# A batch's norm scalars computed on the scalar engine instead of the vector engine

## The reference

```python
def _gn(v, G=32, eps=1e-5):
    g = v.reshape(B_, G, C_ // G, H_, W_)
    m = jnp.mean(g, axis=(2, 3, 4), keepdims=True)
    s = jnp.var(g, axis=(2, 3, 4), keepdims=True)
    return ((g - m) / jnp.sqrt(s + eps)).reshape(v.shape)

def _L0_conv_ref(x, W, b):
    u = jnp.mean(x, axis=1, keepdims=True)
    s = jnp.sqrt(jnp.var(x, axis=1, keepdims=True, ddof=1))
    n_x = (x - u) / (s + EPS)
    n_x = jnp.einsum('bchw,oc->bohw', n_x, W) + b[None, :, None, None]
    return x * n_x

x = x + _L0_conv_ref(_gn(x), L0_conv_W, L0_conv_b)
```

## Time and profile before

| | us |
|---|---|
| median of 3 runs | 1923.73 (1922.91 to 1929.28) |
| the profiled execution | 1922.92 |
| its span, first to last instruction | 1921.1 |

### The profile page before, as it was taken

How to read it: one execution, slowest core, us unless ns; L and a number is a source line. 1 busy time by engine, 2 the same in 40 slices (tenths; PEclk the granted TensorE clock), 3 DMA queues, 4 the chain that set the end, 5 groups by cost and what they waited for, 6 DMA issues and landing times.

```text
span 1921.1 us, 67613 instructions
## 1 busy us (share of the span) xinstructions
PE 1709.8 (89%) x28706; PEld 924.4 (48%) x28706; DVE 1727.3 (90%) x2120; ACT 1434.4 (75%) x2498; POOL 1458.6 (76%) x1684
## 2 busy tenths in 40 slices
PE   0079998999889998999989999899999999899998
PEld 0045554555445554555545555455545555455553
DVE  5669998999899998999989998999989999888887
ACT  5588885888768986888859888588877888544442
POOL 0067877888778887888878887788878888688885
PEclk9989999999999999999999999999999999999999
DMA  9979998999989998999989999899999999845675
GB/s 378 404 292 347 381 387 304 393 391 394 330 322 416 381 399 332 343 400 379 394 312 383 387 392 376 286 408 388 388 348 330 411 376 388 309 188 198 252 276 221
DMA packets 184188, 671.63 MB, mean 350 GB/s; under 512 B 20688, under 2 KB 21072, under 8 KB 183888
## 3 DMA queue, kind: packets, MB, share of 16 engines
q1 hardware_dynamic: 110160, 398.85, 56.1%
q10 hardware_dynamic: 73728, 268.47, 35.0%
HBM read 398.80 MB, written 268.44 MB: 347 GB/s over the span
## 4 chain that ended last, share of the span: by engine, by line
PE 60%; DVE 18%; DMA 10%; issue 6%; POOL 3%; SPq 2%; ACT 2%; POOLq 0%; ACTq 0%; DVEq 0%
PE proj_ps L732 35%; PE sums_ps L720 13%; PE factor_ps L706 11%; DMA tiles<-x 6%; DVE scaled L630 5%; DVE bn L674 4%; DVE bn L675 4%; DMA out<-tiles 4%; SPq L412 2%; DVE tiles L643 2%; POOL tiles L445 1%; POOL tiles L456 1%; DVE gn L584 1%; ACT squares L528 1%; ACT unused L513 0%
## 5 line engine op out<-in xcount | busy, mean ns | idle before, releaser
L732 PE MATMUL proj_ps<-scaled,w_t 128*32 128x512 f32 x8192 | 993.6, 603 | 0.1
L456 POOL TENSOR_SCALAR tiles<-tiles,out_shift 128x1024 f32<-128x1024 f32 x512 | 577.5, 1128 | 241.7 <-DVE tiles L643 239.0
L643 DVE SCALAR_TENSOR_TENSOR tiles<-proj_ps,gate_shift,tiles 128x1024 f32<-128x1024 f32 x512 | 643.8, 1257 | 72.1 <-PE proj_ps L732 70.6
L445 POOL TENSOR_SCALAR tiles<-tiles,norm_scalars 128x1024 f32<-128x1024 f32 x512 | 618.9, 1209 | 58.7 <-DMA tiles<-x 57.7
L513 ACT ACTIVATE unused<-tiles,bn 128x1024 uint8<-128x1024 f32 x560 | 635.0, 1134 | 0.9 <-DMA tiles<-x 0.9
L630 DVE TENSOR_TENSOR scaled<-tiles,factor_ps 128x1024 f32<-128x1024 f32 x512 | 619.3, 1210 | 8.7 <-PE factor_ps L706 3.9
L528 ACT ACTIVATE squares<-tiles 128x1024 f32<-128x1024 f32 x512 | 538.1, 1051 | 112.0 <-POOL tiles L445 66.3
L706 PE MATMUL factor_ps<-pieces,pick_sb 128*128 128x128 bf16 x4096 | 318.1, 221 | 100.8 <-DVE scaled L630 84.6
L720 PEld LDWEIGHTS sums_ps<-tiles,const_sb 128*32 128x32 f32 x8192 | 247.7, 111 | 318.5 <-issue 277.4
L732 PEld LDWEIGHTS proj_ps<-scaled,w_t 128*32 128x32 f32 x8192 | 214.6, 109 | 363.3 <-issue 309.3
L706 PEld LDWEIGHTS factor_ps<-pieces,pick_sb 128*128 128x128 bf16 x4096 | 231.9, 98 | 210.8 <-DVE scaled L630 103.4
(11 more groups left out here) (56 smaller groups left out, 727.4 us busy)
## 6 DMA issues: line engine op xcount, KB each, us to landing
tiles<-x SPq DMA_DIRECT2D x760, 512.0 KB, 10.0
out<-tiles ACTq DMA_DIRECT2D x512, 512.0 KB, 7.0
const_sb<-const SPq DMA_DIRECT2D x1, 193.5 KB, 2.4
scaled<-w SPq DMA_DIRECT2D x1, 64.0 KB, 2.1
scaled<-ident SPq DMA_DIRECT2D x1, 64.0 KB, 2.2
pick_sb<-pick SPq DMA_DIRECT2D x1, 8.0 KB, 2.2
bias_sb<-bias SPq DMA_DIRECT2D x1, 0.5 KB, 2.2
```

What stands on the lines that cost most here:

```text
L445: nc.gpsimd.tensor_scalar(place(s), place(s), norm_scalars[:, 0:1], norm_scalars[:, 1:2], ALU.add, ALU.mult).then_inc(normed, 1)
L456: nc.gpsimd.tensor_scalar(place(s), place(s), 1.0, out_shift[:, 0:1], ALU.mult, ALU.add).then_inc(finished, 1)
L643: nc.vector.scalar_tensor_tensor(out=place(s), in0=proj_ps[:, s % 2, :], scalar=gate_shift[:, 0:1], in1=place(s), op0=ALU.add, op1=ALU.mul ...
L732: mm = nc.tensor.matmul(proj_ps[q:q + 32, s % 2, h:h + BANK], w_t[:, q:q + 32], scaled[:, s % 2, h:h + BANK], start=True, stop=True)
```

## The change

The one-column chain moves to ScalarE, except its first two operations and two reciprocals. VectorE's `gather` (`bn_aggr` and `reduce_sum`) runs at the end of step 58, since `GN_STEP` becomes 58. ScalarE's `moments` (eight operations) runs in step 59 behind the squares and ahead of the store; `deviation` (two) in step 61 behind the root, ahead of the store; `spread_of_group` (eight) in step 62 behind the squares and ahead of the `piece` operations. VectorE's `invert_root` runs in step 62 where part 2 was, and `invert_std` where part 3 was. The two matmuls stay at steps 61 and 62 and read other columns. The epsilon is a column of its own in the constants.

```diff
-        GN_STEPS = 19
-        GN_STEP = slots - 5
+        GN_STEPS = 18
+        GN_STEP = slots - 6
@@ GpSimd, norm, slot 0
                     pool.wait_ge(gn_step, (batch + 1) * GN_STEPS)
+                    pool.wait_ge(inv_std_done, batch + 1)
@@ ScalarE
+            def gn_then(instruction, n, done):
+
+                instruction.then_inc(gn_step, 1)
+                act.wait_ge(gn_step, n * GN_STEPS + done)
+
+            def moments(n, of):
+
+                total = slots * SLOT
+                bn_part = of.bn_slots / slots
+                act.wait_ge(gn_gathered, 2 * n + 2)
+                gn_then(nc.scalar.activation(cell(4), cell(0), ACT.Identity, bias=pivot_of(of), scale=-1.0), n, 1)
+                gn_then(nc.scalar.activation(cell(5), cell(4), ACT.Identity, bias=cell(1), scale=cell(4)), n, 2)
+                gn_then(nc.scalar.activation(cell(6, 2), cell(2, 2), ACT.Copy, scale=1.0 / total), n, 3)
+                gn_then(nc.scalar.activation(cell(8), cell(4), ACT.Identity, bias=cell(6), scale=bn_part), n, 4)
+                gn_then(nc.scalar.activation(cell(9), cell(5), ACT.Identity, bias=cell(7), scale=bn_part), n, 5)
+                gn_then(nc.scalar.activation(cell(10), cell(8), ACT.Copy, scale=-1.0), n, 6)
+                gn_then(nc.scalar.activation(cell(11), cell(8), ACT.Identity, bias=pivot_of(of), scale=-1.0), n, 7)
+                gn_then(nc.scalar.activation(cell(4), cell(8), ACT.Identity, bias=cell(9), scale=cell(10)), n, 8)
+
+            def deviation(n):
+
+                act.wait_ge(group_mean_done, n + 1)
+                gn_then(nc.scalar.activation(cell(5), small_ps[:, 0:1], ACT.Identity, bias=cell(11), scale=-1.0), n, 9)
+                gn_then(nc.scalar.activation(cell(12), cell(5), ACT.Identity, bias=cell(4), scale=cell(5)), n, 10)
+
+            def spread_of_group(n):
+
+                act.wait_ge(group_var_done, n + 1)
+                gn_then(nc.scalar.activation(cell(8), small_ps[:, 1:2], ACT.Relu), n, 11)
+                gn_then(nc.scalar.add(cell(9), cell(8), at["gn_eps"]), n, 12)
+                gn_then(nc.scalar.activation(cell(13), cell(9), ACT.Sqrt), n, 13)
+                gn_then(nc.scalar.activation(neg_mean, small_ps[:, 0:1], ACT.Copy, scale=-1.0), n, 14)
+                if n > 0:
+                    act.wait_ge(out_shift_set, n)
+                gn_then(nc.scalar.activation(mean, small_ps[:, 0:1], ACT.Copy), n, 15)
+                act.wait_ge(gn_inverse_done, n + 1)
+                gn_then(nc.scalar.activation(cell(10), cell(14), ACT.Identity, bias=cell(13), scale=cell(9)), n, 16)
+                gn_then(nc.scalar.activation(cell(15), cell(10), ACT.Copy, scale=0.5), n, 17)
+                if n > 0:
+                    act.wait_ge(gate_shift_set, n)
+                gn_then(nc.scalar.activation(gate_new, cell(15), ACT.Identity, bias=bias_sb[:, 0:1]), n, 18)
...
@@ VectorE (gn_scalars goes)
+            def gather(n, of):
+
+                dve.wait_ge(bn_done, bn_before(n) + of.bn_slots)
+                nc.vector.bn_aggr(gn[:, 0:2], bn_of(of)[:, 0:2 * of.bn_slots, :].rearrange("p a b -> p (a b)"))\
+                    .then_inc(gn_gathered, 1)
+                dve.wait_ge(act_done, act_before(n) + 2 * of.act_slots)
+                nc.vector.reduce_sum(gn[:, 2:4], act_sums[:, :, 0:of.act_slots], AXIS_X).then_inc(gn_gathered, 1)
+
+            def invert_root(n):
+
+                dve.wait_ge(gn_step, n * GN_STEPS + 13)
+                nc.vector.reciprocal(gn[:, 14:15], gn[:, 13:14]).then_inc(gn_inverse_done, 1)
+
+            def invert_std(n):
+
+                dve.wait_ge(gn_step, n * GN_STEPS + 17)
+                nc.vector.reciprocal(inv_std, gn[:, 15:16]).then_inc(inv_std_done, 1)
...
@@ VectorE, gate, slot 0
+                            dve.wait_ge(gn_step, (b + 1) * GN_STEPS)
                             nc.vector.tensor_copy(gate_shift[:, :], gate_new).then_inc(gate_shift_set, 1)
@@ TensorE
-                    if nxt and step == GN_STEP + 2:
-                        pe.wait_ge(gn_step, (b + 1) * GN_STEPS + 9)
+                    if nxt and step == GN_STEP + 3:
+                        pe.wait_ge(gn_step, (b + 1) * GN_STEPS + 8)
...
-                    if nxt and step == GN_STEP + 3:
-                        pe.wait_ge(gn_step, (b + 1) * GN_STEPS + 11)
+                    if nxt and step == GN_STEP + 4:
+                        pe.wait_ge(gn_step, (b + 1) * GN_STEPS + 10)
```

73 lines of the change are left out of this document (19 added, 54 removed).

## The result

The changed kernel takes 1909.87 us in the median of six runs (1906.89 to 1913.88), the kernel before 1923.32 in six beside them (1922.17 to 1929.28): ratio 0.9928, with an interval of 0.9913 to 0.9944. It is faster, by 13.5 us. The profiled execution takes 1910.8 us with a span of 1909.0, 12.1 under the span of before; the forecast was 8.8 under.

The account below looks back on a forecast made before the run. The prediction took TensorE's waits at the seven batch boundaries as what an edit could shorten. Its terms, -12.1 + 2.1 - 1.3 + 3.5 - 3.4 + 2.4, gave -8.8 us: a median of 1915 us, forecast 1908 to 1920, full range 1905 to 1930.

Parts of the forecast that it names:

- Step 60, -12.1: TensorE's gap before step 60, waiting for VectorE's scaled slot, goes whole at all seven boundaries: -12.1 us.
- Steps 54 to 59, +2.1: The gather now stands before step 59's scaling; TensorE waits 1.05 us more at the first and third boundary: +2.1 us.
- Steps 62 and 63, -1.3: VectorE's gain before step 63 is nearly all lost to ScalarE's longer queue before `pieces`: -0.2 us a boundary, -1.3.
- ScalarE's prices: One-column operations on ScalarE: 188 ns without a pointer operand, 108 ns more per pointer, 33 ns between dependent ones.
- The store, +3.5: Step 59's store, issued behind `moments`, delays the last streamed slot's normalization: 0.5 us a boundary, +3.5 us.
- the late store decides: Rival, chance 0.12: the late load and normalization of the last streamed slot at step 62 make the kernel slower, 1932 us.
- The clock, -3.4: Clock falls after the gap before step 60, at three boundaries, 1.7 us each, lose their cause; two counted: -3.4 us.
- the rival that had more of it: Rival, chance 0.14: less idle time also ends the clock falls after load waits just before step 59: 1907 us.
- The start, +2.4: Before the first normalized slot nothing hides the longer chain and the square root's table load of 1.28 us: +2.4 us.
- Given back to DMA (0.19): Rival, chance 0.19: time won at boundaries returns as GpSimd's load waits in steps 54 to 58: 1922 to 1926 us.
- the rival of table loads in each batch: Rival, chance 0.04: two table loads of 1.28 us enter each batch's chain at step 62: 1929 us.
- Two signs of being wrong: GpSimd waiting for the load of the batch's last slot; a gap before step 59 at more than two boundaries.

Follow-up runs that it names:

- moments_back: The changed kernel with the eight operations of `moments` back on VectorE at the end of step 59, the gather left in step 58: 1916.64 us, ratio 0.9961.
- after_again: The changed kernel measured once more, unedited: 1910.84 us, ratio 0.9913.
- reorder: The changed kernel with step 62 reordered on GpSimd, ScalarE and VectorE, the fit's pieces first and `invert_std` behind step 63's scaling: 1896.68 us, ratio 0.9844.
- store_late: The changed kernel with the store of step 59 issued two steps later, behind step 61's squares: 1917.94 us, ratio 0.9969.
- store_first: The changed kernel with the stores of steps 59 and 61 ahead of `moments` and `deviation` in ScalarE's queue: 1908.02 us, ratio 0.9901.
- before_filled: The kernel before with six extra projection matmuls on TensorE in front of step 60's spread: 1924.14 us, ratio 1.0.
- table_early: The changed kernel with one extra one-column square root as ScalarE's first instruction, loading its table early: 1903.11 us in one run.

## Why the prediction was right, and where a term was off

**Step 60, -12.1: right.** The gap went whole at every boundary. The column gives -11.0, since at the seventh the clock fell one step earlier, to 0.71 of 2.4 GHz on the mean of the five us shown above, and step 59 took 4.90 us there instead of 3.28 (+1.6). The second execution doesn't have it (23.0, -12.6 against before). `moments_back` ties the gap to the operations. Part of the gap had a cause that the forecast didn't see: at the fourth and the fifth boundary one operation of the seven took 1.10 and 1.11 us instead of 0.17 (last section).

**Steps 54 to 59, +2.1: +1.2 and +1.5 in the two executions**, in a column with more noise than that. At the first boundary TensorE's wait is 1.21 us where it was 0.71, with VectorE's scaled slot as its releaser: the mechanism is as forecast, with 0.5 us for the 1.05. That releaser stands at the first and the fifth boundary, not the third, and at none in `after_again`. So the gather's price is not measured; the gather alone at step 58 was not tried.

**Steps 62 and 63, -1.3: -1.9.** TensorE starts step 63 at z + 4.66 (z + 4.62 by the prediction's z), against z + 4.7 in the forecast, and GpSimd's `pieces` release it. What I missed on the way is VectorE's idle time before `invert_root`: 2.48 us and not 0.8. I counted it from z, but VectorE is through with its scaling 1.7 us earlier, at 312.07. It costs nothing as long as `pieces` are later than the scaled slot, and `reorder`, in which they are earlier, moves that operation too, so no run shows what it would cost there.

**ScalarE's prices: right within 20 ns.** Groups of ScalarE after, one column with two pointers, with one, and two columns without:

```profile
L535 ACT ACTIVATE gn<-gn 128x1 f32<-128x1 f32 x8 | 3.1, 387 | 0.3
...
L553 ACT ACTIVATE gn<-gn,const_sb 128x1 f32<-128x1 f32 x8 | 2.4, 294 | 0.3
...
L536 ACT ACTIVATE gn<-gn 128x2 f32<-128x2 f32 x8 | 1.6, 203 | 0.3
```

Worked out for one column they were 404, 296 and 188 ns. The page of the Trainium skill named in the prediction, "ScalarE: Activation LUTs" (section "What ACT_TABLE_LOAD costs"), has 93 ns for a pointer; the trace has (387 - 203) / 2 = 92 and agrees.

**The store, +3.5: 0 in the two executions. This is the term that was mis-sized.** The first half of the step holds: the store of step 59 is issued later, at z - 8.8 at the first boundary instead of z - 12.8, and each microsecond behind the limit costs one (`store_late`). The second half failed: I let the 11.95 us from the issue to the normalization shrink by too little. They became 7.33 (7.25 to 9.2 over the boundaries), because the store lands in 2.6 to 4.5 us instead of 4.8 to 7.8 (7.8 in the earlier trace rows). The normalization starts between z - 1.6 and z + 1.18, always inside z + 1.5. `store_first` shows the same from the other side: put back in front, the store takes 5.3 to 8.65 us to land and 10.4 to 12.8 to the normalization, and GpSimd waits for the load at all seven boundaries. The early store's landing thus holds time that a later one doesn't need; what takes that time isn't shown. And the 11.95 us were a poor measure of a latency: in the trace of before GpSimd waits for this load by 0.07 us at the first boundary and not at all at the other six. By the landings of this load, it was there 0.1 to 3.3 us before its normalization, 1.2 on the mean. From the store's issue to the load's landing it is 10.8 us on the mean before and 7.9 after, so of the error the shorter landing of the store is the larger part (6.9 us on the mean before, 3.65 after) and the slack the smaller. The rival "the late store decides" (0.12) had the right place and limit and the wrong latency.

**The clock, -3.4: -3.4 in the first execution, in part by luck.** The three slow steps 60 of 5.21 us are gone (-5.0), and one slow step 59 came (+1.6); the second execution has -5.0 and no slow step 59. That the gap was the cause is supported and not settled. For it: no execution without the whole gap, `before_filled` among them, has a fall in step 60. Against it: before, the clock fell in step 60 behind gaps of 1.91, 1.84 and 1.83 us and not behind those of 1.90 and 1.83, and in `moments_back` none follows the five gaps of 1.30 to 1.47 us. What comes in other steps changes between executions: counted from step 54 on over the seven boundaries, the granted clock falls six times in the trace of before, three times in that of after, and five times in `after_again`, all five in steps 57 and 58. So the rival that had more of it was not borne out by these two. Its 1907 counts from the profiled execution; from the median it would be 1908, the lower end of the forecast's own range.

**The start, +2.4: 2.15 of the column's +2.5.** The first normalization moves from 98.14 to 101.13, 2.99 us, of which 0.84 is a gather that starts later behind its loads (90.06 against 89.22) and not part of the change; from the gather on it is 2.15 us. The table load is exposed for its whole 1.28 us, as `table_early` shows. The chain has one load, at L554 and before the first batch, and none follows in later batches: the rival of table loads in each batch is excluded.

**Given back to DMA (0.19): not seen.** Steps 8 to 54 take 1097.8 and 1097.7 us. GpSimd's waits for loads did grow from 57.7 to 64.9 us, but 5.8 of the 7.2 us stand before the last streamed slot of a batch, inside the limit of z + 1.5, and TensorE pays none of it. It is idle time of an engine with room.

**Two signs of being wrong came and meant nothing.** The prediction named a wait of GpSimd for the load of the batch's last slot: it is there at five of seven boundaries, 0.60 to 2.52 us. And it named a gap before step 59 at more than two boundaries: there are six, two in `after_again`, but the kernel before had five already, and only two of the six are released by VectorE. Both were named without a limit or a releaser, so they couldn't tell right from wrong.

**The sum.** -8.8 forecast and -12.1 found: the store 3.5 too dear, the other terms together found 2.0 more than forecast, and 2.2 went against me in the last batch, where the change does nothing. In medians it is -13.5 against -8.7, with an interval of -16.7 to -10.8, which leaves the -8.7 out. The time lies in the forecast's own range of 1908 to 1920.

**What stays open.** What makes the clock fall at one boundary and not at the next: the falls move between executions of one kernel. What spreads the last batch over 4 us. What the gather's earlier place costs or gives by itself. And how the tail's move is priced in sum: the run meant for it shows 0.26 us a boundary where the load isn't late, and a second effect where it is.

## What to carry to other kernels

Small operations on one column are cheap on either engine (0.15 to 0.4 us each here); what they cost is set by what stands behind them in their engine's queue, so move them off the engine that releases the next step, to one with room, even where each gets slower there (2.6 us instead of 1.9 here, for a gap of 1.2 to 1.9 us that went whole). Then read the three queues around the next wait: putting the two producers of `pieces` ahead of what merely stood before them gave about as much again as the whole change (14.2 us in the median, 10.7 of them in that step's column). And before a transfer's delay goes into a sum, read when it lands, not only when its consumer runs: from before to after the store was issued 5.1 us later against z on the mean and the load behind it landed 2.2 us later, but from after to `store_late` it was 2.1 us and 2.7.

## What the runs showed that I had not expected

A two-column operation on VectorE can end only when a GpSimd operation beside it does. In `moments_back` the operation on two columns, L640, takes 856 ns in the median, and in the kernel before the same one took 193, with 1101 and 1108 at the fourth and the fifth boundary (ns min/median/max):

```profile
L640 DVE TENSOR_SCALAR gn<-gn x8: 170/856/895, 92.4 to 1660.0; 128x2 f32<-128x2 f32 x8
```

```profile
L588 DVE TENSOR_SCALAR gn<-gn x8: 168/193/1108, 91.9 to 1662.6; 128x2 f32<-128x2 f32 x8
```

The second and the fourth boundary of the kernel before; at the second no GpSimd operation ran beside it:

```profile
529.27 0.17 DVE L588 TENSOR_SCALAR gn<-gn 128x2 f32<-128x2 f32 x1
```

```profile
981.42 1.12 POOL L456 TENSOR_SCALAR tiles<-tiles,out_shift 128x1024 f32<-128x1024 f32 x1
981.47 1.10 DVE L588 TENSOR_SCALAR gn<-gn 128x2 f32<-128x2 f32 x1
```

At the first boundary of `moments_back` it ends at 303.31, as GpSimd's 1.12 us operation from 302.17 does (303.29); the one-column operations around it keep their 0.2 to 0.3 us, and on ScalarE the two-column one takes 203 ns at every boundary. Over `before`, `before_filled` and `moments_back` it took over 0.4 us seventeen times, and each time it ended 22 to 26 ns behind the GpSimd operation that was running when it started; in the other seven cases none was running (four) or the one that was ended within 75 ns of its start (three), and it took 168 to 216 ns. So the traces show that it waits for GpSimd; no run was made for it. The Trainium skill's "GPSIMD Engine Reference" (section "1. Specifications") says that GpSimd shares its SBUF interfaces with VectorE and that they contend when VectorE runs in a mode with two ports; that would fit if the operation on two columns ran in such a mode, which no run here shows.

A store that is issued later can land in less time: at the third boundary, with the same 512 KB, it took 8.23 us from z - 10.87 (`store_first`), 4.51 from z - 7.94 (after) and 3.87 from z - 6.12 (`store_late`). On the mean of the seven boundaries it took 6.9, 3.65 and 4.2 us, so the last step is no gain. What holds the early one is not shown.
